# Decoder layer on one core: the clamp of the state-space mixer on VectorE, z's low parts earlier on GpSimd, keys and values ahead of the product with w3 on TensorE

## What is computed

```python
x = layernorm(x) @ w1.T;  x = silu(depthwise_conv3(x))           # width 256
delta = softplus(x @ dl_w.T + dl_b)                               # width 512
A_bar = exp(-delta * (x @ A_w.T + A_b))
h = cumsum((x @ B_w.T + B_b) * cumprod(A_bar))
ssm = h @ C_w.T + C_b + x @ D_w.T + D_b
z = ssm * silu(ssm @ w2.T)
x = x_in + ssm + z @ w3.T
q = layernorm(x) @ WQ + bQ;  k = ctx @ WK + bK;  v = ctx @ WV + bV
```

## Time and profile before

| what | value |
|---|---|
| median of three runs (lowest, highest) | 880.38 us (880.03, 880.54) |
| time of the profiled execution | 886.03 us |
| its span | 884.3 us |
| PE busy | 693.3 us (78%) |
| DVE busy | 578.6 us (65%) |
| ACT busy | 434.1 us (49%) |
| POOL busy | 370.6 us (42%) |
| mean granted TensorE clock | 0.883 of full speed |

### The profile page before, as it was taken

How to read it: one execution, slowest core, us unless ns; L and a number is a source line. 1 busy time by engine, 2 the same in 40 slices (tenths; PEclk the granted TensorE clock), 3 DMA queues, 4 the chain that set the end, 5 groups by cost and what they waited for, 6 DMA issues and landing times. The chain is left out here.

```text
span 884.3 us, 15113 instructions
## 1 busy us (share of the span) xinstructions
PE 693.3 (78%) x4776; PEld 607.0 (69%) x4792; DVE 578.6 (65%) x1269; ACT 434.1 (49%) x971; POOL 370.6 (42%) x338
## 2 busy tenths in 40 slices
PE   3767969799765068898888676516999999999992
PEld 2556858688644046666666575516999999999992
DVE  6574466574753049999999767713777787777741
ACT  4554646535341047777777512103565565555641
POOL 1429456364420300000000156671466866866756
PEclk9788979989997569999999856556999999999997
DMA  9002005511030242121111052215044354251213
GB/s 302 19 25 86 1 24 212 190 65 69 23 111 30 90 139 51 47 46 47 47 46 41 19 197 73 70 43 186 2 136 113 60 147 131 39 146 19 28 22 41
DMA packets 54858, 70.36 MB, mean 80 GB/s; under 512 B 10843, under 2 KB 45542, under 8 KB 54800
## 3 DMA queue, kind: packets, MB, share of 16 engines
q1 hardware_dynamic: 45584, 61.82, 21.7%
q0 software_dynamic: 9216, 7.81, 6.2%
HBM read 42.57 MB, written 28.79 MB: 81 GB/s over the span
## 5 line engine op out<-in xcount | busy, mean ns | idle before, releaser
L1115 ACT ACTIVATE a_pr<-a_scores,a_nm 128x128 f32<-128x128 f32 (+1 forms) x256 | 90.5, 426 | 81.9 <-DVE a_nm L1187 78.6
L1695 DVE SCALAR_TENSOR_TENSOR w_v<-w_th,w_bank 128x324 f32<-128x324 f32 x128 | 63.0, 492 | 70.5 <-ACT w_th L1425 69.2
L1564 PE MATMUL w_bank<-w_w2h,w_hh 128*108 128x256 f32 x384 | 108.5, 283 | 0.5 <-POOL w_hl L1350 0.5
L1564 PE MATMUL w_bank<-w_w2h,w_hl 128*108 128x256 f32 x384 | 107.7, 280 | 0.0
L1564 PE MATMUL w_bank<-w_w2l,w_hh 128*108 128x256 f32 x384 | 107.4, 280 | 0.0
L1425 ACT ACTIVATE w_th<-w_bank 128x324 f32<-128x324 f32 x128 | 56.6, 442 | 100.0 <-PE w_bank L102 99.8
L1350 POOL TENSOR_TENSOR w_hl<-w_v,w_hh 128x324 fp32r<-128x324 f32 x64 | 56.4, 882 | 91.4 <-ACT w_hh L1431 91.4
L1184 DVE TENSOR_REDUCE a_mx<-a_scores 128x2 f32<-128x512 f32 (+1 forms) x96 | 65.5, 682 | 35.6 <-remote 34.1
L1366 POOL IOTA w_x<- 128x16 uint32 x1 | 0.2, 190 | 208.0 <-POOLq L1078 208.0
L102 PE MATMUL w_bank<-w_xh,w_w1h 128*128 128x324 f32 x256 | 81.1, 317 | 1.1 <-ACT w_xh L1420 1.1
L102 PE MATMUL w_bank<-w_xh,w_w1l 128*128 128x324 f32 x256 | 80.8, 316 | 0.0
(11 more groups left out here) (230 smaller groups left out, 2031.2 us busy)
## 6 DMA issues: line engine op xcount, KB each, us to landing
w_s<-in_L_ffn_w SPq DMA_DIRECT2D x16, 1024.0 KB, 5.9
disp<-c_blank SPq DMA_DIRECT2D x8, 658.1 KB
w_rows<-disp SPq DMA_DIRECT2D x8, 658.1 KB
vd<-m_vs SPq DMA_DIRECT2D x4, 816.0 KB, 3.7
a_vs<-vd SPq DMA_DIRECT2D x1, 3264.0 KB, 11.8
g_x<-in_x SPq DMA_DIRECT2D x4, 512.0 KB, 7.7
m_cin<-in_ctx SPq DMA_DIRECT2D x4, 512.0 KB, 5.0
kd<-m_qkh SPq DMA_DIRECT2D x4, 512.0 KB, 2.9
```

Source lines behind the costliest of these rows:

```text
L1115: ins = act.activation(pr[:, u % 2, j * n:(j + 1) * n], sbank[u % 3][:, j * n:(j + 1) * n], ACT.Exp, bias=nm[:, u, j:j + 1], scale=SCALE)
L1564: mm = pe.matmul(eb[t // 2][0:SP_, (t % 2) * D:(t % 2 + 1) * D], a[:, g % 3, s], w2_piece(b, f), start=f == 0 and t % 2 == 0 and n == 0, s ...
L1695: dve.scalar_tensor_tensor(v[:, n % 4, :], th[:, n % 2, :], 1.0, hb[n % 3][:, 0:HALF], ALU.add, ALU.mult).then_inc(F["v"], 1)
```

## The change

The clamp `dmin` leaves POOL's queue and is done on DVE, with its four calls placed in DVE's order of work: ahead of the low part of q, between delta 0 and delta 1, ahead of running 1, and between weighted 1 and running 2. On POOL the order becomes ssm_sum, ssml, g_low 0, z_low 0 and 1, g_low 1 to 3. On ACT exp 3 moves behind z's high parts. On PE, keys and values go ahead of w3, and mixed 1 ahead of turn_q. In PAIRS, W3 moves behind K and V, and the waits that guard the pairs follow: mixed waits for both value evictions (vf), w3 for the low part of k (kl), keys for z, and values no longer for x_out. On DVE, the low part of k and the value additions go ahead of residual, statistics and normed of the block before; summed 0 comes behind normed.

```diff
--- before.py
+++ after.py
@@ -164,7 +164,7 @@
 HIGH_ORDER = ("w1", "dl_w", "A_w", "B_w", "D_w", "WQ", "w2", "WO")
 LOW_VECTOR = ("w1", "dl_w", "A_w", "B_w", "D_w")
 LOW_GPSIMD = ("WQ", "w2", "WO")
-PAIRS = ("Q", "T", "D", "W1", "W2", "TC", "W3", "K", "V", "C", "TQ")
+PAIRS = ("Q", "T", "D", "W1", "W2", "TC", "K", "V", "W3", "C", "TQ")
 
 
 def mixer_and_projections(nc, sems, c, x_sb, wo, bo, a, disp, qd, kd, vd):
@@ -328,11 +328,6 @@
                     pool.wait_ge(S["ve"], n)
                     pool.tensor_tensor(rstd[:, s], ve[:, s], c["mhalf"][:, s], ALU.pow).then_inc(S["rstd"], 1)
 
-                def dmin(i, m):
-                    n = HC * i + m
-                    pool.wait_ge(S["dexp"], n + 1)
-                    pool.tensor_scalar(e[:, n % 2, :], e[:, n % 2, :], BIG, None, ALU.min).then_inc(S["dmin"], 1)
-
                 def ssm_sum(i, m):
                     pool.wait_ge(S["hs"], DC * i + m + 1)
                     pool.wait_ge(S["dx"], DC * i + m + 1)
@@ -372,9 +367,6 @@
                     if last and now:
                         ssm_sum(i - 1, 0)
                         ssm_sum(i - 1, 1)
-                    if now:
-                        dmin(i, 0)
-                        dmin(i, 1)
                     if last and now:
                         ssml(i - 1, 0)
                         ssml(i - 1, 1)
@@ -387,9 +379,6 @@
                         split_done(pool, "D_w")
                     if now:
                         g_low(i, 0)
-                        dmin(i, 2)
-                        g_low(i, 1)
-                        dmin(i, 3)
                     if i == 0:
                         for m in vs:
                             pool.memset(m[:, :], 0.0).then_inc(S["vzero"], 1)
@@ -401,6 +390,7 @@
                         z_low(i - 1, 0)
                         z_low(i - 1, 1)
                     if now:
+                        g_low(i, 1)
                         g_low(i, 2)
                         g_low(i, 3)
                     if i + 1 < NBLK:
@@ -603,11 +593,11 @@
                         x_tanh(i + 1, 1)
                     if now:
                         act.preload_act_table_set("natural_log_exp_and_others")
-                        exp(i, 3)
                     if last:
                         z_high(i - 1, 0)
                         z_high(i - 1, 1)
                     if now:
+                        exp(i, 3)
                         g_high(i, 1)
                         log(i, 3)
                         c_high(i)
@@ -685,7 +675,7 @@
                 def mixed(i, m):
                     pe.wait_ge(S["gh"], HC * (i + 1))
                     pe.wait_ge(S["gl"], HC * (i + 1))
-                    pe.wait_ge(S["kl"], DC * (i + 1))
+                    pe.wait_ge(S["vf"], 2 * (i + 1))
                     split_product(pe, pair(i, "C", m)[:, :], products("C_w", m, (gh, gl))).then_inc(S["C"], 1)
 
                 def w2(i):
@@ -703,6 +693,7 @@
                         pe.wait_ge(S["identr"], 1)
                     pe.wait_ge(S["zh"], DC * (i + 1))
                     pe.wait_ge(S["zl"], DC * (i + 1))
+                    pe.wait_ge(S["kl"], DC * upto(i + 2))
                     for n in range(2):
                         for j in range(2):
                             tok = slice((2 * n + j) * P, (2 * n + j + 1) * P)
@@ -725,11 +716,11 @@
                         split_done(pe, "WQ")
                     pe.wait_ge(S["ch"], DC * (i + 1))
                     pe.wait_ge(S["cl"], DC * (i + 1))
+                    ge(pe, S["z"], DC * i)
                     for m in range(DC):
                         split_product(pe, pair(i, "K", m)[:, :], products("WK", m, (xbh, xbl))).then_inc(S["k"], 1)
 
                 def values(i):
-                    ge(pe, S["x_out"], 2 * i)
                     pe.wait_ge(S["dx"], DC * (i + 1))
                     for n in range(2):
                         for j in range(2):
@@ -775,16 +766,16 @@
                         turn_c(i)
                         chunk(i, "B", 2)
                         chunk(i, "B", 3)
+                    if now:
+                        keys(i)
+                        values(i)
                     if last:
                         w3(i - 1)
                     if now:
-                        keys(i)
-                        values(i)
                         mixed(i, 0)
+                        mixed(i, 1)
                     if last:
                         turn_q(i - 1)
-                    if now:
-                        mixed(i, 1)
 
             @block.vector
             def _(dve):
@@ -846,6 +837,11 @@
                 def silu(i, m):
                     dve.wait_ge(S["th"], DC * i + m + 1)
                     dve.scalar_tensor_tensor(cv[:, m, :], th[:, m, :], 1.0, cv[:, m, :], ALU.add, ALU.mult).then_inc(S["silu"], 1)
+
+                def dmin(i, m):
+                    n = HC * i + m
+                    dve.wait_ge(S["dexp"], n + 1)
+                    dve.tensor_scalar(e[:, n % 2, :], e[:, n % 2, :], BIG, None, ALU.min).then_inc(S["dmin"], 1)
 
                 def delta(i, m):
                     n = HC * i + m
@@ -952,16 +948,19 @@
                 for i in range(NBLK + 2):
                     now, last = i < NBLK, 0 <= i - 1 < NBLK
                     if now:
-                        delta(i, 0)
+                        dmin(i, 0)
                     if i >= 2:
                         biased_low(i - 2, "Q", bq, i)
                     if now:
+                        delta(i, 0)
+                        dmin(i, 1)
                         delta(i, 1)
                     if i + 1 < NBLK:
                         x_low(i + 1)
                     if now:
                         running(i, 0)
                         weighted(i, 0)
+                        dmin(i, 2)
                         running(i, 1)
                     if i == 0:
                         dve.wait_ge(S["x2"], 16 * (NBLK - 2))
@@ -983,6 +982,7 @@
                         gated(i - 1, 1)
                     if now:
                         weighted(i, 1)
+                        dmin(i, 3)
                     if last and not now:
                         for m in range(DC):
                             last_low("zl", zl, z, zh, "zh", i - 1, m)
@@ -999,18 +999,17 @@
                         weighted(i, 2)
                         running(i, 3)
                         weighted(i, 3)
+                    if now:
+                        biased_low(i, "K", bk, i)
+                        value(i, 0)
+                        value(i, 1)
                     if last:
                         residual(i - 1, 0)
                         residual(i - 1, 1)
                         dve.wait_ge(S["x_out"], 2 * i)
                         statistics(st2, mom2, ve2, TPB * (i - 1), TPB * i)
-                    if now:
-                        biased_low(i, "K", bk, i)
-                    if last:
                         normed(i - 1)
                     if now:
-                        value(i, 0)
-                        value(i, 1)
                         summed(i, 0)
                     if i == NBLK - 1:
                         last_sum(i, 0)
```

## The result

The changed kernel took 888.91 us (median of 4 runs, 887.82 to 889.72), the kernel before 880.20 (4 runs): ratio 1.0098, 95% interval 1.0081 to 1.0116. It is slower by 8.7 us where 17.5 us less were forecast. The profiled execution took 889.72 us, its span is 887.7 us.

What follows compares the result with a forecast made beforehand. It took TensorE's idle time in the first phase as the limit. Block gains and the tail's loss gave -19.0 us, plus 1.5 for the port: 17.5 off the 880.38 median, so 862.9 us, range 857 to 868 (chance 0.60).

Steps and rivals of the forecast that it cites:

- Part 1: First phase: 16 clamps move from GpSimd, 1.48 us each, to VectorE, 0.42 each, adding 6.7 us there.
- A port: VectorE and GpSimd hold each other up: clamps caught at two places beside GpSimd work, 1.5 us taken, 7.5 at worst.
- Part 3: TensorE, keys and values ahead of w3: same work, hole some 3.4 us instead of 5.83, w3 waits 0 to 1.1.
- part 2: Last clamp of a block: context's low part 2.1 us earlier; waits for z's low parts end at about 174.1.
- Part 4: End of a block: residual, statistics, power and normed covered by mixed products; TensorE waits about 1.1 us before the queries.
- the sum of 5.6 us: Time between w3 and the normed rows: residual, statistics, power and normed, 0.7 + 2.2 + 1.1 + 1.4.
- The tail: After the last block: transposes now come last, so the last sum ends some +2.3 us later relative to the block's end.
- The slower case: End of a block: late value remainders, x2's high part and summed 1 make queries wait in four blocks; 885 us, chance 0.04.

Runs made afterwards that it cites:

- e3: Changed kernel with the TensorE order undone (w3 ahead of keys and values as before), clamp on VectorE and z's low parts early: 866.25 us, ratio 0.9817.
- e8: e3 with z's low parts behind g1's on GpSimd and exp 3 ahead of z's high parts on ScalarE, so only the clamp moved: 866.45 us.
- e1: Changed kernel with the value remainders ahead of the power in GpSimd's queue, no longer beside normed: 877.07 us, ratio 0.9953.
- e4: e1 with z's low parts on GpSimd made to wait for the scan of group 2 and both silu: 876.01 us, ratio 0.9918.
- e7: Kernel before with the new TensorE order alone, clamp left on GpSimd, and value remainders ahead of the power: 890.76 us, ratio 1.0085.
- e6: Changed kernel with the value remainders on GpSimd made to wait until normed is done, queue order unchanged: 885.73 us, ratio 1.0041.

## Why the prediction was wrong, point by point

- **Part 1 and its place in block 0** were right in kind: the waits on the clamp went (41.0 to 4.2 us), 16 clamps cost 6.8 us plus holds, and block 0 gained 4.0 us of the 7.2 forecast (6.4 in e3). The clamp alone gains 15.5 us (e3, e8). The signs that the prediction gave, blocks starting near 78, 128 and 181 and the last low part of q near 267, are met by e3 (78.3, 128.1, 182.3, 268.9), not by the changed kernel (80.2, 135.5, 194.8, 290.8). In part that is luck, since e3 carries 13.8 us of hold on scans and clamps that the sum had at 1.5.
- **"A port" is the first term that failed, the order of parts 3 and 4 the second.** The measured median is 26.0 us above the forecast: 11.8 go with the place of the value remainders beside normed (the changed kernel against e1), 10.8 with the order itself (e1 against e3), 3.4 are left (e3 against 862.9). The port was priced at 1.5 us in all, with 7.5 as the worst, because it asked only where a *clamp* could be caught. What is caught are old instructions whose neighbours on GpSimd changed: the scans took 31.2 us instead of 20.5 (+10.7), normed 15.5 us instead of 5.5 (+10.0), the clamps 9.3 instead of 6.8 (+2.5), together 23 us of hold on VectorE. Not all of that is lost time: the scans' and the clamps' part stands in e3 too, which gains 15.5 us all the same; it is normed's part that the slower kernel has and e3 has not. The Trainium skill's page SBUF — State Buffer, in the section on who interferes with whom, names VectorE instructions with two SBUF operands beside the 2-port ones; the trace agrees: the scan, which reads two operands from SBUF, went from 1.26 to 3.36 us. The prediction cited the section for the clamp alone, though the row that it held against it (the 128x4 operation of 3.43 us) is itself one with two operands from SBUF.
- **Part 3** said that the order is free and the hole shrinks to 3.4 us. The hole was 5.3 us in blocks 1 and 2 and 3.9 in block 3, since the scan's 2.1 us of hold lie on the chain to the context's low part; in e4, where that scan is free, it is 3.07 us. w3's wait for kl, put at 0 to 1.1 us, did not come. Worse, part 2 itself found z's low parts ready at 174.1, but the prediction never asked what the *old* order would then do. e3 answers it: w3 first, 866.25 us. The order costs 9 to 11 us even with the remainders moved away from normed (e7, e1), where the sum had it as free but for w3's wait and the tail.
- **Part 4** had the sum of 5.6 us (its four terms add up to 5.4) "just covered" by two mixed products. With normed at 4.7 us it was 8.9, from the end of w3 at 184.89 to the end of normed at 193.79 in block 2, so the transposes waited in three blocks and the next block began at the low clock. The tail was put at +2.3 and measured +6.3: the queries' wait went from 1.45 to 3.60, as forecast, but the low clock on the products behind it took the other 4.
- **The rivals.** The slower case, at 4 in 100, had its place right, the end of the block, and its time near (885). It put the cause in the value remainders *standing ahead* of x2. That is part of it: e1 takes them out of both places and wins 12 us, e6 takes them only away from *beside* normed and wins 3 to 5. But its sign, a wait of about 5 us ahead of the queries in each block, did not come; the changed kernel has one such wait, 3.60 us, and otherwise waits for normed.

## What to carry to other kernels

When work leaves one of VectorE and GpSimd or changes its place, list for each stretch what the other runs at that moment, and price every VectorE instruction of the kinds that were held here (the scan, the statistics, normed and the clamp, all from SBUF) at up to one whole GpSimd instruction, not only the instruction that is moved. Test the parts of a change one by one: here a gain of 15 us and a loss of 20 stood in one diff. When a product's input becomes ready earlier, its old place may already be the best, so work out the old order with the new times before changing both. And a piece of work moved to be ready earlier can cost its gain again by whom it now runs beside, as z's low parts do beside the scan (e3 and e8).

## What the runs showed of the hardware that was not expected

Back-to-back VectorE instructions lost their turn each time: four normed instructions, 1.38 us together when free, ran beside four GpSimd ones of some 1.17 and took 4.71 us, and the transposes that they released started 1.16 us apart (191.54, 192.70). Small instructions were held as long as large ones: 128x4 operations went from 0.16 to 1.2 us. It shows as busy time, so a VectorE that looks busier (607.8 us of the span instead of 578.6) may only be waiting.
